# A four-layer selective-scan kernel: new last stages, maps loaded in bands, smaller first loads of the scans, and products of delta and u moved to GpSimd

## The reference, cut to what matters

```
x_dbl = xs @ x_proj                      # dt (rank 6), B (16), C (16) at every point
delta = softplus(dt @ dt_proj + bias)
h = h * exp(delta * A) + (delta * u) * B # for every channel and state, point after point
y = sum over states of h * C, + D * u
```

## Time and profile before

| what | us |
|---|---|
| median of three runs | 29121.85 (29090.61 to 29128.26) |
| the profiled execution, its own time | 29087.84 |
| span of its instructions | 29086.0 |
| four scans, each | 5383 to 5393 |
| `prepare` in layers 0, 2, 3 | 566.8, 562.1, 569.6 |
| `prepare_causal`, layer 1 | 946.4 |
| `finish_ln` in layers 0, 3 | 369.7, 368.9 |
| `finish` in layers 1, 2 | 213.6, 234.6 |

### The profile page before, as it was taken

How to read it: one execution, slowest core, us unless ns; L and a number is a source line. 1 busy time by engine, 2 the same in 40 slices (tenths; PEclk the granted TensorE clock), 3 DMA queues, 4 the chain that set the end, 5 groups by cost and what they waited for, 6 DMA issues and landing times. The chain is left out here.

```text
span 29086.0 us, 327672 instructions
## 1 busy us (share of the span) xinstructions
PE 23153.7 (80%) x96912; PEld 6785.5 (23%) x96912; DVE 25421.4 (87%) x16276; ACT 14595.5 (50%) x20071; POOL 22864.1 (79%) x10240
## 2 busy tenths in 40 slices
PE   8878888886666888888868788888856788888885
PEld 3322222221232222222234222222212322222222
DVE  3489999999478999999966899999994799999995
ACT  1255555554266555555504555555532655555551
POOL 0169999998046999999952799999960499999991
PEclk9878888887766888888858888888877788888887
DMA  2242222223454222222175322222235522222215
GB/s 84 102 134 48 47 44 44 47 48 91 135 196 151 48 48 44 43 47 48 40 248 209 105 44 43 47 48 48 48 132 182 182 48 48 48 48 48 48 40 179
DMA packets 1156880, 2420.85 MB, mean 83 GB/s; under 512 B 118490, under 2 KB 656058, under 8 KB 1143732
## 3 DMA queue, kind: packets, MB, share of 16 engines
q1 hardware_dynamic: 1155004, 2398.41, 29.8%
HBM read 1374.98 MB, written 1023.05 MB: 82 GB/s over the span
## 5 line engine op out<-in xcount | busy, mean ns | idle before, releaser
L1545 POOL TENSOR_TENSOR scan_hc<-scan_bc,scan_h 128x1024 f32<-128x1024 f32 x6912 | 16096.3, 2368 | 110.5 <-DVE scan_h L1709 94.8
L1709 DVE TENSOR_TENSOR_SCAN scan_h<-scan_da,scan_state,scan_dbu 128x1024 f32<-128x1024 f32 x6912 | 15988.3, 2338 | 141.3 <-ACT scan_da L1597 133.9
L1628 PE MATMUL scan_da<-scan_dd,scan_ssel 32*128 32x512 f32 x27648 | 9099.9, 745 | 3010.0 <-DVE scan_h L1709 2775.9
L1597 ACT ACTIVATE scan_da<-scan_da,scan_a_cur 128x1024 f32<-128x1024 f32 x6912 | 7516.2, 1087 | 7723.7 <-PE scan_da L1628 7717.8
L1628 PE MATMUL scan_p_du<-scan_dd,scan_ssel 32*128 32x512 f32 x27648 | 9201.4, 745 | 538.0 <-DMA scan_bc<-bc_d 212.0
L1696 DVE TENSOR_TENSOR scan_dbu<-scan_p_du,scan_bc 128x1024 f32<-128x1024 f32 x4608 | 5561.8, 1207 | 501.0 <-PE scan_p_du L1628 468.8
L1531 POOL TENSOR_TENSOR scan_dbu<-scan_bc,scan_dus 128x1024 f32<-128x1024 f32 x2304 | 5458.8, 2369 | 145.7 <-ACT scan_dus L1571 144.6
L1628 PEld LDWEIGHTS scan_da<-scan_dd,scan_ssel 32*128 32x128 f32 x27648 | 2450.8, 216 | 10300.0 <-DVE scan_h L1709 8736.7
L1645 PE MATMUL scan_p_y<-scan_hc,scan_rsel 128*32 128x512 f32 x27648 | 4775.3, 772 | 16.6 <-POOL scan_hc L1545 16.6
L1628 PEld LDWEIGHTS scan_p_du<-scan_dd,scan_ssel 32*128 32x128 f32 x27648 | 2410.5, 211 | 3617.2 <-DVE scan_dbu L1696 2969.9
L1576 ACT ACTIVATE scan_state<-scan_h,scan_a_cur 128x1 f32<-128x1 f32 x6912 | 2022.9, 293 | 1585.0 <-DVE scan_h L1709 1476.7
(11 more groups left out here) (216 smaller groups left out, 13571.6 us busy)
## 6 DMA issues: line engine op xcount, KB each, us to landing
scan_bc<-bc_d SPq DMA_DIRECT2D x576, 512.0 KB, 12.1
du_d<-prep_useq SPq DMA_DIRECT2D x384, 576.0 KB, 4.0
delta_d<-prep_delta SPq DMA_DIRECT2D x384, 576.0 KB, 4.3
scan_dd<-delta_d SPq DMA_DIRECT2D x1152, 192.0 KB, 4.8
scan_dd<-du_d SPq DMA_DIRECT2D x1152, 192.0 KB, 6.5
y_d<-scan_y SPq DMA_DIRECT2D x576, 384.0 KB, 5.2
merge_y<-y_d SPq DMA_DIRECT2D x384, 576.0 KB, 5.6
xs_d<-proj_xs_o SPq DMA_DIRECT2D x96, 588.0 KB, 3.3
```

Source lines behind the costliest of these rows:

```text
L1545: nc.gpsimd.tensor_tensor(hc[:, u % HC_SLOTS, :], c, h[:, u % H_SLOTS, :], ALU.mult).then_inc(hc_ready, 1)
L1597: nc.scalar.activation(da[u % DELTA_BANKS][:], da[u % DELTA_BANKS][:], ACT.Exp, scale=a_cur[:, slot(u)[0], u % UNITS:u % UNITS + 1]).then_ ...
L1628: return nc.tensor.matmul(dst[:, half * H:(half + 1) * H], ssel[rows, i, :], dd[rows, s, m, j, :], start=True, stop=True)
L1709: nc.vector.tensor_tensor_scan(h[:, v % H_SLOTS, :], da[v % DELTA_BANKS][:], dbu[:, v % DBU_SLOTS, :], state[:, v % UNITS:v % UNITS + 1], ...
```

## The change

In `prepare` GpSimd makes the products and the resets, between walks: the first two chunks are walked ahead, and the walk of chunk c + 2 stands behind the first product of chunk c. VectorE keeps cap and softplus; softplus also waits for the product three steps back. The map is loaded in eight bands of 12 rows, three ahead and one more after each pair. So that the first eight chunks need one band each, layer 2, whose walks begin with columns, makes its row walks first (`TURN`), and writes each chunk to its old place. `prepare_causal` loads bands of 8 rows. The scan loads what its first eight units need first, then the rest of the slot; ScalarE issues the constants, of which A comes once a direction, not once a chunk. `finish_ln` is deeper by a stage: square sums spread over all partitions by nine matmuls of 128 columns, 64-row and 64-column matmuls for tile 2, and two images in two banks. `finish` has four slots and two PSUM buffers.

```diff
 prepare
-                for m in range(TILES):
-                    sp.dma_start(grid[:, m, :], map_d[:, m, :]).then_inc(grid_loaded[m], 16)
+                load_band(0)
...
+                for c in range(1, 3):
+                    load_band(c)
...
+                    if v // 2 + 3 < CHUNKS:     # at the end of SyncE's pair v, v + 1
+                        load_band(v // 2 + 3)
             @block.gpsimd
+                def times_u(v):
+                    g.wait_ge(delta_ready, v + 1 + ONE)
+                    g.tensor_tensor(piece(v), delta[:, v % SLOTS], piece(v), ALU.mult).then_inc(du_ready, 1)
+                def reset(v):
+                    first = -(v % PIECES) * N % WINDOW
+                    g.wait_ge(du_ready, v + 1 + ONE)
+                    g.memset(delta[:, v % SLOTS, :, first::WINDOW], RESET_DELTA).then_inc(reset_done, 1)
+                for c in range(2):
+                    walk_chunk(c)               # waits for grid_loaded[c], du_stored of chunk c - 3
+                for v in range(STEPS):
+                    times_u(v)
+                    if l == 0:
+                        reset(v)
+                    c = v // PIECES + 2
+                    if v % PIECES == 0 and c < ALL:
+                        walk_chunk(c)
             @block.vector
                 def softplus(v):
                     d.wait_ge(log_done, v + 1 + ONE)
                     d.wait_ge(delta_stored[v % SLOTS], 16 * (v // SLOTS) + ONE)
+                    d.wait_ge(du_ready, max(v - SLOTS + 1, 0) + ONE)
...
-                        times_u(v + b)
-                        if l == 0:
-                            reset(v + b)
 prepare_causal
-                    sp.dma_start(grid[:, m, :], map_d[:, m, :]).then_inc(grid_loaded[m], 16)
+                for j in range(AHEAD):          # 4 bands; one more for each pair i, from i + 2 * AHEAD = 4
+                    load_band(j)
 scan
+                def load_first():
+                    for j in range(2):          # delta and product: one tile, blocks 0 and 1
+                        for n, src, half in sources:
+                            sp.dma_start(dd[rows, 0, 0:1, j, :], ...).then_inc(first_loaded, 16)
+                    for r in (0, IMAGES):       # B and C of image 0
+                        sp.dma_start(bc[:, 0, r, :], ...).then_inc(first_loaded, 16)
...
+                        if first and u == FIRST_UNITS - TRIO:      # TensorE, unit 5
+                            t.wait_ge(loaded[0], LOADS + ONE)
-                t.wait_ge(loaded[0], LOADS + ONE)
+                t.wait_ge(first_loaded, FIRST_LOADS + ONE)
+                a.dma_start(a_dir[:], w["alog"]).then_inc(consts, 16)
 finish_ln
                 def square_sum(s):
                     for m in range(TILES):
-                        last = nc.tensor.matmul(p_v[:, 0:N], mean[:, m, :], sq[:, m, :], ...)
+                        for j in range(TILES):
+                            last = nc.tensor.matmul(p_c[:, j, N:512], mean[:, m, :], sq[:, m, j * PIECE:(j + 1) * PIECE], ...)
                 def spread(s):
+                        rows = slice(m * QUAD, (m + 1) * QUAD) if m < 2 else slice(HALF, P)
+                        nc.tensor.matmul(p_r[:, m, 0:N], gamma[rows, :], rs[rows, :], ...)
                 def centre_y(s):
+                    t.wait_ge(dev_ready, s + ONE)
+                    for b in range(IMAGES):     # full, then rows = a half, then cols = a half, then full
+                        nc.tensor.matmul(p_c[:, b, 0:N], centre[:, 0, :], y[:, b, :], start=True, stop=False)
...
-                for s in range(STEPS + 2):
+                for s in range(STEPS + 3):      # square_sum(s - 1), spread(s - 2), centre_y(s), project_out(s - 3)
 finish
-        ym = ph.sb("ym", [P, 2, TILES, N])
+        DEEP = 4
+        ym = ph.sb("ym", [P, DEEP, TILES, N])
+        p_o = [ph.ps(f"p_o{j}", [CH, IMAGES, 512]) for j in range(2)]
+                for s in range(STEPS + 1):      # VectorE
+                    if s < STEPS:
+                        gate(s)
+                    if s >= 1:
+                        add(s - 1)
```

458 lines of the change are left out of this document (228 added, 230 removed).

## The result

The changed kernel takes 28589.5 us, median of 4 runs (28564.2 to 28605.8), beside 29107.1 for the kernel before (4 runs on the same chip, 29090.6 to 29128.3): a ratio of 0.9821, with a 95% interval from 0.9804 to 0.9838. The forecast was 28490, with a range from 28360 to 28690. So it is faster, by 1.8%, and inside the range, but 100 us behind the forecast. The profiled execution took 28586.77 us (span 28585.0), 501 less than the 29087.84 of before; the forecast's sum was 628.

What follows compares the result with a forecast made beforehand. VectorE and GpSimd fill the four untouched scans; the edited stages between are mostly chains of waits. Savings 116 + 75 + 25 + 84 + 192 + 140 - 4 = 628 us from 29087.84 give 28490 on the median's scale, range 28360 to 28690.

Steps and rivals of the forecast that it cites:

- rival A: Delta's making: GpSimd bounds all of it, so the loops give nothing; 28606 us, chance 0.17.
- Products to GpSimd: Delta's making, layers 0, 2, 3: moving 96 products a layer off VectorE saves 116 us (bounds 20 to 170).
- D's ring: Delta's making: store, softplus, product and walk waits close into a ring, chain and GpSimd run serially; 29921 us, chance 0.02.
- The undisturbed chain: Delta's making: softplus, caps, Exp, table load and Ln take 9.5 us a pair of steps, 14.25 a chunk.
- so TensorE is late next: Delta's making: with products gone the cap waits for TensorE's expansion, so 0.84 us of 1.47 is gained a pair.
- Bands: Delta's making: loading the map in bands starts TensorE earlier; 75 us over layers 0, 2, 3, and 25 in layer 1.
- Scan beginnings: Start of the four scans: waiting for 1.57 MB instead of a whole slot saves 21 us each, 84 (bounds 60 to 92).
- The cover: Scan beginnings: the slot's rest arrives at 29.8 us, before TensorE asks at 34; slower transfers could remove this margin.
- Norm stages: Last stages of layers 0 and 3: a step falls from 14.02 to 10.0 us, saving 192 us in all.
- Rival B: Last stages with a norm stay bound by TensorE: halves don't overlap, short passes pay their loads; 28682 us, chance 0.12.
- Last stages of layers 1 and 2: Four slots and two PSUM buffers leave DMA bounding at 5.75 us a step; saves 140 us (bounds 100 to 154).
- the first rule weighed in the prediction: Walks: GpSimd contends with VectorE instructions having two SBUF inputs, so stalls go; if they stayed, some 100 us more.

Runs made afterwards that it cites:

- e4: Changed kernel with even steps' products and resets of layers 0, 2, 3 on GpSimd, odd ones on VectorE behind the caps; 28565.2 us (0.9817).
- e7: Changed kernel, products on GpSimd, with four slots each for delta and the walked input in layers 0, 2, 3; 28448.4 us (0.9774).
- e1: Changed kernel with products and layer 0's resets of layers 0, 2, 3 back on VectorE in their old place; 28584.7 us (0.9822).
- e12: e7 with all twelve of layer 1's map bands issued at the stage's beginning, ahead of the stores; 28446.6 us (0.9776).
- e6: Changed kernel with products and resets of layers 0, 2, 3 on VectorE behind the caps, four slots for delta and walked input; 28497.7 us (0.9788).
- e11: Changed kernel with full matmuls instead of pairs of halves in the last stages of layers 0 and 3; 28611.2 us, one run.
- e8: e6 with the three matmuls of each odd step's projection issued twice; 28539.0 us (0.9804).

## Why the prediction was right, and where it was not

The mechanism was right in most parts and wrong in one, and the time is inside the range partly by luck: the range had been widened over rival A's time (28606), and the forecast's own range ended at 28590, 0.5 us above what was measured. The sum was 127 us too large, nearly all of it in one term.

**Products to GpSimd: 116 forecast, nothing measured.** This is the step that failed, and rival A's outcome is what this part had, though not for A's reason: e4 and e7 show that GpSimd's load wasn't the bound with three slots. The sentence that failed is "I followed the order through three pairs and found every such wait met early". It was D's ring in a mild form. I had taken 3.4 us from a store of `du` to the walk that needs its slot; over layer 2's sixteen column walks it is 5.4 us on average and 6.6 in the median from the product's end to the walk. They take turns: in every second one the store is issued at once and the walk begins after 3.4 to 4.3 us; in the others (6.6 to 6.8 us, as in the rows above) it first stands on SP behind others for 1.9 us and then lands in 4.9. In layer 2 a column chunk took 17.3 us and not 15.6 (pairs of 11.53), a row chunk 15.3 and not 14.25 (pairs of 10.23). e7 gives the price of the slots: with one more of each kind the same scheme saves the 131 us, and its pairs are 9.86 us where the forecast had 9.95. The undisturbed chain of the forecast was right, and the buffers under it were one short. That the means agree is in part luck: the forecast had 9.5 in row walks and 10.4 in column walks, e7 has 9.8 to 9.9 in both, since slow expansions lengthen the one and GpSimd no longer stands idle for the landing in the other.

**The clock of the expansion.** The forecast's pair came from one expansion of 3.08 us. In e7 a pair takes 9.49 us where the expansion takes 2.84, and is longer by just what the expansion is longer: 10.36 with 3.71, 12.12 with 5.48 (at 0.50 of the clock). That is 0.37 us a pair on average (9.86 against 9.49), the rest of the distance to 9.5. The forecast had "so TensorE is late next" and didn't ask at which clock. It also set its undisturbed 9.5 against a mean of 10.8 in which slow expansions were contained. In the kernel before VectorE's product ahead of the caps hid a little of them, but in layers 2 and 3 the 28 pairs with an expansion over 3.5 us took 11.6 on average, the 55 with an undisturbed one 10.35. So "because VectorE's products are longer beside a walk" was only a part of the reason for 10.8.

**Bands: 75, measured 83** by e1. Layer 1: 25 forecast, 16.7 measured. Its VectorE works without a pause 32 us sooner, and later waits 4 us for a first tap because a band stands on SP behind a pair's stores; e12 removed that wait for 9 us.

**Scan beginnings: 84, measured 75.5.** The start itself is right: the first scan instruction (VectorE, the recurrence) comes 21.2 us into layer 0's stage and not 42.9, 21.6 saved in each. The bodies vary: over the twelve later runs, all with these scans, the four sum to 21456 to 21473 us, so the saving is 72 to 90. Layer 0's, which saved only 9.9 here, saved 22.8 in e6. The cover held: in the 80 us from layer 0's start TensorE waits for a transfer once, at the beginning.

**Norm stages: 192, measured 180.** Step 10.35 against 10.0: square sums 2.2 (2.5), spread 1.7 (1.5), centring 4.1 (3.5), ScalarE 2.35 (2.45). The square sums' 18 passes, each with a weight load, take 2.27 us: they start 0.112 apart, and a third of a 384-column pass (0.322) is 0.107, so their loads are hidden and the forecast's 2.5 had paid for them in part. The pairs of halves take 0.84 and 0.80, as the earlier trace rows had them. What was mis-sized is the price of a change of tiling mode. The forecast read it off as at most 0.16 us and took it to be inside the 0.80. The trace has it on both sides of each change: where full matmuls and halves meet, the last pass ahead of the change and the first behind it are each followed after 0.41 to 0.43 us and not 0.32. So such a change costs 0.2 us, and half of it falls on the full matmuls beside a pair (1.49 us for the two of L2227, 0.75 for L2235). From the end of the square sums to the end of the centring there are six changes, by estimate 1.1 us of the 10.35. Rival B, that halves don't overlap and short passes pay their loads, is excluded by e11 and by the 0.112.

**Last stages of layers 1 and 2: 140, measured 158.** The step is 5.9, bound by loads at 300 GB/s; the forecast had 5.75 and 294. The gain is larger since the steps of before averaged more than the 8.5 of the two in the earlier trace rows: 213.56/24 is 8.9.

**The walks' stalls** went, as the first rule weighed in the prediction has it. No copy in layer 2 takes longer than 1.24 us now (1.52 in e7), where the longest was 2.36; in e6, with the products back on VectorE, it is 2.35 again and a product takes up to 3.45. But one reading was wrong. The walk of the earlier trace rows at 15745.60, called one without a product beside it, had one: the product stood still in its place, 4.13 us where it takes 1.35.

```profile
15749.44 4.13 DVE L1097 TENSOR_TENSOR prep_useq<-prep_delta,prep_useq 128x1152 f32<-128x1152 f32 x1
```

## What to carry to other kernels

When work moves from one engine to another, count the slots again: from the instruction that frees a slot to the one that refills it goes the whole way through the issuing queue and the store's landing, and work that is now queued behind a waiting instruction lengthens every ring that runs through it. Read a wait on a slot back to what holds the slot: the fourth delta slot, which VectorE seemed to ask for, gave nothing in layers 2 and 3, and the fourth input slot gave most (68 of the 85 us that both gave there). If there is room for one more slot of each kind, try it ahead of any new order: here it was worth 131 us in these stages (28448 against 28590 as a whole), when four other orders of the same work (e1 to e4) were worth 35 at most. And where a mean is set against an undisturbed case, ask what the mean contains: here it was TensorE's expansions at half the clock.

## What the runs showed of the hardware

- Two stretches in which TensorE is busy 0.95 and 0.97 of the time were granted 0.83 (layer 0's delta in e8) and 0.99 of its clock (layer 0's last stage). In the first the clock goes from 1.00 to 0.50 behind an expansion, at 1501.3, with TensorE idle for 0.64 of the 6.7 us ahead of it.
- Nine matmuls of 128 columns, 18 passes, take 2.27 us and start 0.112 apart, beside weight loads of 0.116 on average (127.92/1104 in that stage's window): short passes did not pay for their loads in addition.
- A change between full matmuls and halves costs 0.2 us at the full clock: 0.1 on the pass ahead of it and 0.1 on the pass behind it, with 384 columns 0.41 to 0.43 us from start to start and not 0.32 (layer 0's last stage, 19 steps alike).
- A VectorE product with both inputs in SBUF and a GpSimd walk hold each other up: the product took 4.13 us and not 1.35 at 15749.44, the walk of three copies 4.56 us and not 3.4 at 15760.72.
- A `du` store of 576 KB landed in 4.0 us (median over all layers) in the kernel before, in 4.7 in the changed one and in 4.9 in e7, whose stages of layers 0, 2 and 3 moved 240 to 243, 251 to 258 and 274 to 278 GB/s. That the traffic is the cause was not tested.
